# Cross-attention scores in two paired passes, another order of the pipeline's steps, and the first expert's weights loaded beside the first stores

## What is computed

```python
x = x + attn(layernorm(x))           # 16 heads of 16, causal window of 64
x = x + xattn(layernorm(x), ctx)     # 16 heads of 16, 375 keys, relative position bias
x = x + ffn(layernorm(x))            # 8 experts, 256 -> 512 -> 256, top 2 of 8

# xattn
q = hidden @ Wq ; k, v = split(ctx @ Wkv)
scores = einsum('bhsd,bhkd->bhsk', q, k) + bias
out = einsum('bhsk,bhkd->bshd', softmax(scores), v) @ Wo
```

## Time and profile before

| | |
|---|---|
| median of 3 runs | 1296.43 us (1296.26 to 1296.63) |
| the profiled execution | 1294.94 us, of which the span is 1293.2 |
| TensorE busy | 1221.5 us, 94% |
| VectorE, ScalarE, GpSimd busy | 67%, 56%, 66% |
| both attentions and the router | 0 to about 905 us |
| expert network | from about 931 us |
| mean granted TensorE clock | 0.98 |

### The profile page before, as it was taken

The page is one execution under the profiler, slowest core; times in us unless marked ns, Lnnn a source line. Parts: engine busy times, 40 slices in busy tenths (PEclk is TensorE's granted clock), DMA queues, the critical chain, the costliest instruction groups (busy, mean ns, idle before and its releaser), DMA issues. The chain is left out here.

```text
span 1293.2 us, 39996 instructions
## 1 busy us (share of the span) xinstructions
PE 1221.5 (94%) x13786; PEld 1084.2 (84%) x13787; DVE 869.6 (67%) x3942; ACT 726.3 (56%) x1822; POOL 851.0 (66%) x1595
## 2 busy tenths in 40 slices
PE   6899999999999999999999999996199999999996
PEld 4688888888888888888888888885199999999996
DVE  3567778787787877888778787786344444444443
ACT  3466666666666666666666666664054444444442
POOL 4677787887878878778787887765434444444443
PEclk8999999999999999999999999998599999999998
DMA  8700011100110111100111110101377322233222
GB/s 165 134 21 22 28 39 44 29 29 28 39 44 29 28 29 39 44 29 29 29 39 44 29 28 24 33 16 30 126 217 180 50 48 44 47 49 49 49 46 25
DMA packets 43957, 66.22 MB, mean 51 GB/s; under 512 B 6833, under 2 KB 30769, under 8 KB 43793
## 3 DMA queue, kind: packets, MB, share of 16 engines
q1 hardware_dynamic: 27808, 38.93, 11.4%
q0 software_dynamic: 15552, 25.05, 10.0%
q10 hardware_dynamic: 432, 0.10, 0.0%
HBM read 43.10 MB, written 20.95 MB: 50 GB/s over the span
## 5 line engine op out<-in xcount | busy, mean ns | idle before, releaser
L480 POOL TENSOR_SCALAR arena<-arena,mC 112x375 f32<-112x375 f32 x512 | 299.1, 595 | 117.6 <-DVE mC L888 117.4
L888 DVE CUSTOM_DVE_ANT_0 arena<-bank_S,arena 112x375 f32<-112x375 f32 x512 | 264.9, 543 | 90.7 <-PE bank_S L612 64.1
L1124 POOL DMA_INDIRECT out<-y,xb x63 | 114.8, 1822 | 206.2 <-DVE y L1270 165.4
L486 POOL TENSOR_SCALAR arena<-arena,mF 112x112 f32<-112x112 f32 x512 | 176.8, 362 | 23.1 <-DVE mF L876 21.4
L770 ACT ACTIVATE pTC<-bank_Q 126x336 f32<-126x336 f32 x286 | 128.6, 450 | 45.8 <-PE bank_Q L622 44.5
L734 ACT ACTIVATE arena<-bank_B 128x224 f32<-128x224 f32 (+5 forms) x229 | 87.5, 382 | 109.9 <-PE bank_B L541 35.1
L1257 DVE SCALAR_TENSOR_TENSOR hT<-bankU,gub,gate 128x128 f32<-128x128 f32 x252 | 71.0, 345 | 105.8 <-PE bankU L1166 93.7
L734 ACT ACTIVATE arena<-bank_A 128x224 f32<-128x224 f32 (+3 forms) x219 | 82.3, 376 | 96.7 <-PE bank_A L635 28.4
L622 PE MATMUL bank_Q<-ident,arena 112*126 112x112 f32 x858 | 130.9, 261 | 0.5 <-ACT pTC L770 0.5
L1166 PE MATMUL bankG<-xbT,gwb 128*128 128x128 f32 x1008 | 124.7, 277 | 1.0 <-ACT gwb L1213 1.0
L1207 ACT ACTIVATE xbT<-bankX 128x256 f32<-128x256 f32 x63 | 24.2, 384 | 178.1 <-PE bankX L1154 178.1
(11 more groups left out here) (207 smaller groups left out, 2919.3 us busy)
## 6 DMA issues: line engine op xcount, KB each, us to landing
arena<-in_l_ctxT SPq DMA_DIRECT2D x32, 378.0 KB, 3.6
xb<-xs POOLq DMA_DIRECT2D x63, 129.0 KB, 3.4
arena<-in_L_ffn_gate_w SPq DMA_DIRECT2D x8, 512.0 KB, 4.7
arena<-in_L_ffn_up_w SPq DMA_DIRECT2D x8, 512.0 KB, 5.7
arena<-in_L_ffn_down_w SPq DMA_DIRECT2D x8, 512.0 KB, 3.9
arena<-in_x SPq DMA_DIRECT2D x32, 112.0 KB, 2.2
out<-arena SPq DMA_DIRECT2D x32, 112.0 KB, 1.9
arena<-skew SPq DMA_DIRECT2D x8, 328.1 KB
```

The source lines that it names most:

```text
L480: pool.tensor_scalar(z[n % NZ][:, 0:T], z[n % NZ][:, 0:T], -1.0, mC[:, n:n + 1], ALU.mult, ALU.add).then_inc(s_u, 1)
L486: m = pool.tensor_scalar(sF[r][:, j, :], sF[r][:, j, :], -1.0, mF[:, r, j:j + 1], ALU.mult, ALU.add)
L888: dve.tensor_tensor_reduce(out=z[n % NZ][:, 0:T], in0=bank[f"S{r}"][0:S, 0:T], in1=nbias[:, n, :], scale=1.0, scalar=3.0e38, op0=ALU.add, ...
L1124: pool.indirect_dma_start(out=out[:, :], out_offset=bass.IndirectOffsetOnAxis(ap=xb[x][:, D + 1:D + 2].bitcast(I32), axis=0), in_=y2[x % 2 ...
```

## The change

- **Scores.** The cross score group has two passes. In a tile of 32 rows, head p of the pair has its high keys in the rows of parity p and its low keys in the rows of the other parity (`k2[:, c, p, :]`). The first pass multiplies by the high queries, standing in both parities, the second by the low queries in both. The columns of Wq and Wkv are ordered so that a pair's heads alternate row by row (`lay_out`), for the self-attention as well.
- **Copies.** `keys_high` writes the high keys twice (one copy for each p), and the low keys go to a buffer of their own, `k2_low`, of which there is one. `halves` multiplies by the constant -1 in place of the mask.
- **Transfers.** Two new steps on SP's queue, `kx` and `qx`, of two DMAs each: they copy the low keys, and the high and low queries, to the rows of the other parity, from SBUF to SBUF. `cross_scores` waits for both (`s_kx`, `s_qx`) in place of the drained banks; the subtraction into `k2_low` waits until the `kx` of the sequence before has landed.
- **Order.** `PERIOD` is another list, with other shifts.
- **Weights.** The first expert's weights are loaded behind the stores of sequences 0 and 1, in two halves, and not ahead of the padding rows.

```diff
--- before.py
+++ after.py
@@ -53,7 +53,7 @@
     i, j = np.arange(S)[:, None], np.arange(S)[None, :]
     window = np.where((j <= i) & (j > i - WINDOW), 0.0, -MASKED).astype(np.float32)
     half_mask = np.zeros((P, 2), np.float32)
-    half_mask[np.arange(P), np.arange(P) // DH % 2] = -1.0
+    half_mask[np.arange(P), np.arange(P) % 2] = -1.0
     before = (i < j).astype(np.float32)
     return {
         "c_one_hot": one_hot, "c_window": window, "c_half_mask": half_mask, "c_before": before,
@@ -64,14 +64,14 @@
 
 
 PERIOD = """
-rs1@3 sT0@3 e15@-1 t15 u14@-1 pv2@1 u12@-1 q2l@1 t14 t12 ln1@4 e13@-1 x3@-2 k1c@1 u13@-1 st@-2 t13 rcB@-2 t2@1
-t1@1 t3@1 e3 oc3@-1 xn@3 km@2 u1 u3 t0@1 x3Tc@-2 u2 Lc@2 rs3@-2 e2 pfD@-2 onc@1 pv1@1 e1 t4@1 e0 S0@2 cl@2
-k0c@1 t6@1 e7 t5@1 nrm@2 oncc@-1 e6 t7@1 k1l@2 pf@-1 u0 oc0 u6 u4 u7 u5 sc@-3 e4 p14@1 re@-2 xn2@1 u8 v0@2 e9
-e10 x2Tc@1 Lx@5 sT1@3 p12@1 e8 S1@2 pvS@3 u9 xTc@3 u10 u11 e5 v@4 rs2@1 p15@1 q2m@1 p13@1 qkc@3 e11 ot@3 t11@1
-t10@1 k1@3 sE2@2 nrmc p3@2 t8@1 pv3@1 t9@1 v1c@1 S2@2 k0l@2 sE3@2 x1@2 x3T p2@2 su3@2 ln2@2 oc2 on@3 sm3@3
-p1@2 otc@1 lg@-1 sE0@2 su2@2 p0@2 oc1 sm2@3 k0@3 x2 sm1@3 sm0@3 wo@3 p7@2 p6@2 su0@2 u15 ln3 onC@1 S4@4 pv0@2
-rcA@-1 e14 v0c@1 sE1@2 rt p4@2 woc@1 p9@2 p10@2 ch@2 x2T@3 xT@5 p8@2 p5@2 e12 oTc@2 q2@3 S3@2 qk@5 p11@2 sT2@4
-v1@3 vc@3 sT3@4 su1@2
+oTc@1 qx@-1 S0 km@3 u9 rt@-3 Lc@2 p11@-1 p8@-1 woc@-2 e7@-1 e10@-1 v@2 st@-3 oc0@-1 p9@-1 on@1 e11@-1 re@-3 kx
+p13@-1 pv1@-1 t10 u14 S4@2 rs1@5 e8@-1 p14@-1 vc@2 e9@-1 xT@3 onc@1 e13@-1 wo@1 qk@3 oc1@-1 u15 xTc@3 e14@-1
+u3@1 k1@1 u2@1 p15@-1 sT0@2 pv2@-1 rs3@-1 S1 p12@-1 nrmc@-1 u12 x3@-2 su0@3 t14 qkc@3 x3T@-2 k1c@1 k0@1 t12 p3
+t15 t13 Lx@4 u1@1 e15@-1 sE0@2 sT3@2 su1@3 v1@1 su3@3 p1 pv3@-1 S2 rs2@2 p2 u6@1 x2T@1 oc2@-1 pf@-3 e12@-1
+x3Tc@-2 sT1@2 sT2@2 q2@1 cl@2 su2@3 k0c@1 p0 ln1@5 nrm@2 t2@1 lg@-2 t3@1 e3 xn2@1 p6 v0@1 sE3@2 otc@-1 t0@1 u0@1
+e1 x2@-1 p4 S3 ln3@-1 t1@1 rcA@-2 p5 onC@-1 sm0@3 v1c@1 oc3@-1 p7 sm1@3 u4@1 u7@1 pvS@2 u5@1 x1@2 e2 u11@1
+x2Tc@1 u8@1 sm2@3 sm3@3 ln2@2 sE1@2 k1l@2 t5@1 sE2@2 t7@1 pv0 u10@1 q2m@1 t6@1 sc@-2 p10 t4@1 e6 e0 v0c@1 k0l@2
+rcB@-2 e4 t9@1 ch@2 xn@4 t11@1 pfD@-2 t8@1 u13@1 q2l@2 oncc@-1 ot@2 e5
 """
 
 
@@ -234,8 +234,9 @@
             cT = [s1(f"cT_{part}", [P, DC, TPAD], F32R) for part in ("high", "low")]
             wkv = [s1(f"wkv_{part}", [P, DC, 2 * D], F32R) for part in ("high", "low")]
             PASSES = ((0, 0), (1, 0), (0, 1))
-            q2 = [[s1(f"q2_{part}{i}", [P, DC, 2, S], F32R) for part in ("high", "low")] for i in range(2)]
-            k2 = [[s1(f"k2_{part}{i}", [P, DC, T + 1], F32R) for part in ("high", "low")] for i in range(2)]
+            q2 = [s1(f"q2_{i}", [P, 2, DC, 2, S], F32R) for i in range(2)]
+            k2 = [s1(f"k2_{i}", [P, DC, 2, T + 1], F32R) for i in range(2)]
+            k2_low = s1("k2_low", [P, DC, T + 1], F32R)
             v2 = [sa([TP, TC, H, HP]) for i in range(2)]
             z = [sa([S, TPAD]) for i in range(NZ)]
             mC = s1("mC", [S, H])
@@ -323,6 +324,8 @@
 
             s_qh = sem("cross_queries_high_ready")
             s_kh = sem("cross_keys_high_ready")
+            s_kx = [sem("cross_keys_paired0"), sem("cross_keys_paired1")]
+            s_qx = [sem("cross_queries_paired0"), sem("cross_queries_paired1")]
 
             NLATE = 8
 
@@ -413,9 +416,6 @@
                     for b in range(3, NX):
                         load_x(b)
                     load_c(1)
-                    for half in range(2):
-                        load_package(sp, 0, half)
-
                     sp.wait_ge(s_pad0, 1)
                     sp.dma_start(xs[E * R:E * R + P, :], pad[:, :]).then_inc(s_spare, 16)
 
@@ -426,9 +426,22 @@
                         elif step == "Lc" and b >= 2:
                             need(sp, s_cl, b - 1)
                             load_c(b)
+                        elif step == "kx":
+                            drained_wait(sp, "k0", b)
+                            drained_wait(sp, "k1", b)
+                            for p in range(2):
+                                sp.dma_start(k2[b % 2][1 - p:P:2, :, p, :].bitcast(F32),
+                                             k2_low[p:P:2, :, :].bitcast(F32)).then_inc(s_kx[b % 2], 16)
+                        elif step == "qx":
+                            drained_wait(sp, "q2", b)
+                            for p in range(2):
+                                sp.dma_start(q2[b % 2][1 - p:P:2, :, :, p, :].bitcast(F32),
+                                             q2[b % 2][p:P:2, :, :, p, :].bitcast(F32)).then_inc(s_qx[b % 2], 16)
                         elif step == "st":
                             drained_wait(sp, "woc", b)
                             sp.dma_start(out[b * S:(b + 1) * S, :], x2[b % 2][:, :]).then_inc(s_st[b % 2], 16)
+                            if b < 2:
+                                load_package(sp, 0, b)
                     sp.wait_ge(s_pad, 16 * E)
                     sp.wait_ge(s_spare, 16)
                     for q in range(2):
@@ -603,15 +616,13 @@
                         m.then_inc(F_, 1)
 
                     def cross_scores(g, b, F_):
-                        if g == 0:
-                            drained_wait(pe, "q2", b)
-                        drained_wait(pe, f"k{g // 2}", b)
-                        c, k = g // 2, g % 2
-                        for u, w in PASSES:
+                        need(pe, s_qx[b % 2], 32 * (b // 2 + 1))
+                        need(pe, s_kx[b % 2], 32 * (b // 2 + 1))
+                        c, p = g // 2, g % 2
+                        for u in range(2):
                             for r in range(HG):
-                                m = pe.matmul(bank[f"S{r}"][0:S, 0:T + 1], q2[b % 2][u][32 * r:32 * r + 32, c, k, :],
-                                              k2[b % 2][w][32 * r:32 * r + 32, c, :],
-                                              start=(u, w) == PASSES[0], stop=(u, w) == PASSES[-1])
+                                m = pe.matmul(bank[f"S{r}"][0:S, 0:T + 1], q2[b % 2][32 * r:32 * r + 32, u, c, p, :],
+                                              k2[b % 2][32 * r:32 * r + 32, c, p, :], start=u == 0, stop=u == 1)
                         m.then_inc(F_, 1)
 
                     def probs_back(n, b, B_, F_):
@@ -746,19 +757,19 @@
 
                     def halves(b):
                         B_ = filled_wait(act, "q2", b)
-                        if b == 0:
-                            act.wait_ge(s_mask, 32)
-                        elif b >= 2:
+                        if b >= 2:
                             filled_wait(act, "S3", b - 2)
                         for p in range(2):
-                            m = act.activation(q2[b % 2][0][:, :, p, :], v3(B_, DC, S), ACT.Copy, scale=hmask[:, p:p + 1])
+                            m = act.activation(q2[b % 2][:, 0, :, p, :], v3(B_, DC, S), ACT.Copy, scale=-1.0)
                         m.then_inc(s_qh, 1)
 
                     def keys_high(o, b):
                         B_ = filled_wait(act, f"k{o}", b)
                         if b >= 2:
                             filled_wait(act, "S3", b - 2)
-                        act.activation(k2[b % 2][0][:, o, :], B_[:, 0:T + 1], ACT.Copy).then_inc(s_kh, 1)
+                        for p in range(2):
+                            m = act.activation(k2[b % 2][:, o, p, :], B_[:, 0:T + 1], ACT.Copy)
+                        m.then_inc(s_kh, 1)
 
                     def cross_probs(n, b):
                         B_ = filled_wait(act, f"p{n}", b)
@@ -979,14 +990,16 @@
                         elif step == "q2l":
                             need(dve, s_qh, b + 1)
                             for p in range(2):
-                                m = dve.scalar_tensor_tensor(q2[b % 2][1][:, :, p, :], v3(bank[place["q2", b][0]], DC, S), hmask[:, p:p + 1],
-                                                             q2[b % 2][0][:, :, p, :].bitcast(F32), ALU.mult, ALU.subtract)
+                                m = dve.scalar_tensor_tensor(q2[b % 2][:, 1, :, p, :], v3(bank[place["q2", b][0]], DC, S), -1.0,
+                                                             q2[b % 2][:, 0, :, p, :].bitcast(F32), ALU.mult, ALU.subtract)
                             m.then_inc(drain_sem("q2", b), 1)
                         elif step in ("k0l", "k1l"):
                             o = int(step[1])
                             need(dve, s_kh, kh_count[f"k{o}c", b] + 1)
-                            dve.tensor_tensor(k2[b % 2][1][:, o, :], bank[place[f"k{o}", b][0]][:, 0:T + 1],
-                                              k2[b % 2][0][:, o, :].bitcast(F32), ALU.subtract).then_inc(drain_sem(f"k{o}", b), 1)
+                            if b:
+                                need(dve, s_kx[(b - 1) % 2], 32 * ((b - 1) // 2 + 1))
+                            dve.tensor_tensor(k2_low[:, o, :], bank[place[f"k{o}", b][0]][:, 0:T + 1],
```

(3 more changed lines are left out.)

## The result

The changed kernel takes **1308.1 us** (median of 4 runs, 1306.85 to 1308.27); before it was 1296.35 (4 runs, 1294.63 to 1296.63). The ratio is 1.0088 (95% interval 1.0073 to 1.0102): 0.9% slower, where 1272.8 was forecast, 35 us too low. The profiled execution (1308.04 us, span 1306.4) shows where they are.

The account below looks back on a forecast made before the run. TensorE was taken to bound the steady stretch (busy 828.9 of 836.0 us). Pass -21.8, pvS's wait -6.0, new waits +1.5, start +5.4 and end -2.7 gave -23.6, so 1296.4 became 1272.8 us; range 1264 to 1287.

Parts of the forecast that it names:

- The third pass: Cross score groups on TensorE: dropping one of three passes saves 0.17 us in each of 128 groups, 21.8 us.
- the estimate was 28 us: Rival for the score groups: a pass costs 0.22 us by the packing rule, saving 28 us, total 1266.6; chance 0.02.
- pvS's wait: Self-attention values on TensorE: the 0.2 us wait per period for the bank pfD drains late goes, saving 6 us.
- Copies and transfers: Extra ScalarE/VectorE copies and the kx, qx transfers: hidden, cost 0; qx lands in 2.5 us, with 1.4 us spare.
- The rival that had the other sign: Rival 2: pairs land late, TensorE waits at S0 every period, slower above 4.7 us landing; chance 0.14, 0.08 of it slower.
- The start: Before the steady stretch: S0(0) waits for qx(0) until 52.5 us; with later waits +5.4 us, ends 1 and 9.
- Order in the steady stretch: Reordered steps change TensorE's sum only through waits: 6 us gone, 1.5 us put back, period some 26.0 us.
- small new waits: Steady stretch: 0.05 us a period put back for new waits, 1.5 us; ends 0 and 0.5 a period (15 us).
- the terms' own ends: Limits set for start (1 to 9), new waits (0 to 15) and end (0 to -3.7), given as 1266 to 1281.
- my 26: First period at the start, set by GpSimd and VectorE: 26 us, TensorE's steps some 18, its wait some 1.7.
- The end: After the last score group: nine additional TensorE steps fill idle time, tail 20.4 to 21.4 us, net -2.7 us.

Follow-up runs that it names:

- three_passes: x3_scatter_early's order with x(3) early, but three passes, no pairs or copies between partitions, expert's first weights in their old place; 1296.66 us, ratio 1.0012.
- weights_at_start: x3_scatter_early with the first expert's weights (1.6 MB) in their old place, ahead of the loop on SyncE's queue; 1278.35 us, ratio 0.9862.
- order_alone: The kernel before with only the change's order of operations: three passes, no copies between partitions, expert's first weights in their old place; 1324.69 us, ratio 1.0210.
- x3_scatter_early: The changed kernel with x(3) loaded ahead of the bias table and GpSimd's scatter moved from behind u13 to ahead of u8; 1277.05 us, ratio 0.9849.
- scatter_later: The changed kernel with only the scatter moved in GpSimd's order from ahead of u13 to behind u14, some 3 us later; 1319.66 us, ratio 1.0175.
- cl_later: The changed kernel with x(3) loaded early and VectorE's subtraction cl some 3 us later, behind ln1 and nrm, scatter left in place; 1292.88 us, ratio 0.9984.
- extra_beside_scatter: The kernel before with an extra VectorE subtraction (112x750) 1 us behind the issue of GpSimd's second scatter, beside k0 and wo; 1313.66 us, ratio 1.0126.
- pv0_behind_S0: The changed kernel with x(3) loaded early and pv0 moved behind S0 and rt, scatter left in place; 1327.99 us, ratio 1.0244.
- copies_from_pool: x3_scatter_early plus two plain copies (112 rows of 1032 bytes) from GpSimd's queue where the scatter had stood; 1272.71 us, ratio 0.9819.

## Why the prediction was wrong

The forecast's own landmarks are S0(0) at 52.5 and, with -23.6 us on 905.3, the end of the last `pf` at 881.7, 21.4 behind S3(31) at 860.3. In the change's profile the start is 12.2 us late (64.7), S0(0) to S3(31) 15.2 us longer (823.1 for 807.8), S3(31) to the end of the last `pf` 7.5 longer (28.9 for 21.4), and what follows 1.9. Together 36.8 us between the profiles and 35.3 between the medians, since the forecast set the median 1.5 above its profile.

- **The third pass: right in the group, mis-sized in the sum.** The group takes 0.53 us, so 0.17 us a pass stands, from start to start, and a factor of 4 for four K=32 matmuls, not the 3.07 that the Trainium skill gives ("TensorE: Matmul & The Clock Gate", "Part 3: Packing small matmuls"), by which the estimate was 28 us. But of 0.68 us a period only 0.57 arrives, 17 us for the forecast 21.8 (three_passes against weights_at_start; order_alone against the change has 0.56). The rest stands in `v1` (0.85 us for 0.80) and the step behind it (0.44 for 0.38); why was not tried. That three_passes and x3_scatter_early lie 21 us apart is luck: the weights' place adds what is missing.
- **pvS's wait: right.** It is gone.
- **Copies and transfers: right.** In the steady stretch TensorE never waits for a pair; 188 KB of `kx` land a median 2.3 us after issue, and 112 KB of `qx` (in the runs whose profile gives it) 2.2 to 2.6, for 2.5 forecast. The rival that had the other sign failed.
- **The start: failed.** I followed SyncE's queue to qx(0), and not VectorE's order, where `nrm(0)` now stands behind the statistics of x(3). I knew that x(3) was late and left out who waits for it. With x(3) early, and nothing else, S0(0) starts at 51.6, behind the q pair as forecast. That is 13 us, shown.
- **Order in the steady stretch: failed, in "small new waits".** I looked for waits by semaphore and put back 1.5 us, with 15 as the end. (That end was left out of the range: the terms' own ends add up to 1266 to 1293, not 1281.) The loss was 17 us (stretch of the change 823.1, of x3_scatter_early 805.7), in a gap that no dependency explains. Shown: it goes when the scatter moves away (x3_scatter_early, scatter_later), and when `cl` moves away (cl_later); it comes with the order alone; plain transfers don't cause it; and in two other places the two operations don't cause it, under `k0` and `wo` (extra_beside_scatter) and under `p10` and `ot` (pv0_behind_S0). The condition that fits all runs is threefold: an indirect scatter just issued, a large VectorE operation on two SBUF arrays, and the run of 24 short matmuls beside it. How many matmuls it takes, and what the three share, stays open. Without the gap the stretch is 2.1 us shorter than I had it; the first periods (21.3, 24.3, 25.4 us) were better than my 26.
- **The end: mis-sized.** It had -2.7 us; the length was to be 21.4 (7.3, 13.4 and the 1.0 us of the last `pf` itself make 21.7). TensorE's timeline from the last group on:

```profile
887.75 0.60 PE L624 MATMUL bank_S<-k,q 32*112 32x376 f32 x8 [1.17 <-DVE mC L899]
...
889.19 1.35 PE L646 MATMUL bank_A<-pTC,arena 126*32 126x112 f32 x24
...
895.84 0.82 PE L646 MATMUL bank_B<-pTC,arena 126*32 126x112 f32 x24
...
899.92 0.78 PE L646 MATMUL bank_A<-pTC,arena 126*32 126x112 f32 x24 [0.41 <-ACT pTC L781]
...
910.30 0.61 PE L540 MATMUL bank_A<-ident,arena 112*128 112x112 f32 x2 [3.92 <-ACT arena L755]
...
915.66 0.51 PE L654 MATMUL bank_B<-chosen,before 112*112 112x8 f32 x2 [3.38 <-DVE chosen L913]
```

`pv3` starts 12.2 us behind S3, not 7.3. TensorE has waited 1.17 us for S3; then the granted clock is 0.98 for 1.4 us and 0.50 (1.2 GHz) from `pv0` (889.19) to `pv1` (895.84), and these eight steps take 6.65 us; the same steps take 3.6 in the steady stretch (`pv0` without its gap). From `pv1` to `pv3` 1.6 us more go by than their steps, 0.9 of it in waits for ScalarE's copies. From `pv3` on the chain takes 15.7 us and not 13.4, at a granted clock of 0.59 for 0.72 before. My sum had the steps and neither the clock nor the waits between them. The clock is not all of it: in x3_scatter_early the same eight steps take 4.2 us at 0.86, and its tail is still 26.5 us for the 20.4 of the forecast (21.4 less the last `pf`). No run isolates this part; it comes with the order in order_alone (28.0), and in the other kernels of this order it is 25.0 to 30.0.

x3_scatter_early, the change with both repairs, beats both: 1277.05 us, 1.5% below before, and 4 us above the forecast. In part that nearness is luck: its start (50.2) and its stretch (805.7) are 2 us shorter each than the forecast's, its end is 6 us longer.

## What to carry to other kernels

A pass taken off the bound engine is worth its time only if the order can use it: here the old order turned the 0.17 us into waits, and the new one was level with the old until it had the shorter groups. When steps are reordered, follow each engine's queue at the start too, and ask of every step that moved ahead what it waits for and who stands behind it. And don't believe a time that hits its number before the rows show the same mechanism: extra_beside_scatter came out at 1313 for another reason than the one that had foretold it.

## What the runs showed of the hardware

- TensorE lost about 0.7 us, with no semaphore in it, in a run of short matmuls beside an indirect scatter and a large VectorE operation. The cause inside the chip stays open; that TensorE runs short of instructions there is a rival that no run tried. GpSimd's next operation is slowed by the same `cl`: 1.22 us (613.98) for 0.59 alone, in periods without a gap as well. The Trainium skill ("SBUF — State Buffer", "Terms") says that VectorE and GpSimd lock a port pair against each other; the row agrees. It adds that TensorE has ports of its own, so that rule doesn't account for TensorE's gap. The Trainium skill, "DMA: Bandwidth & Descriptors", section "SWDGE vs HWDGE vs iDMA", says that GpSimd writes the descriptors of plain and indirect transfers alike, into SBUF state that VectorE locks it out of in its 2-port mode; if TensorE's gap came from that, copies_from_pool should have had it too, and it had none.
- copies_from_pool does more than x3_scatter_early and comes out 0.3% faster (the intervals overlap). In the profiles the first expert block is waited for 23.5 us and not 26.2. Whether the two transfers a period shorten this wait, and how, wasn't tried.
- In the change, where TensorE waited 16.1 us for x(3), its granted clock was 0.50 (1.2 GHz) from 25 to 50 us; with x(3) early it is 0.82 from 25 to 51.5.
